# Last layer's end reordered in a four-layer attention stack: mixing, second keys, gating's last quarter, negated maxima, and the place of the loop edge

## What is computed

```python
kt = conv1x1(x, w_qk, b_qk)              # 1024 pixels
qt = conv1x1(xp, w_qk, b_qk)             # 256 pooled pixels
vt = conv1x1(xp, w_v, b_v)
pi = softmax(mix_weight @ mean(kt), over the 2 parts of a head)
attn = softmax(kt, over the 16 channels of a part) @ vt
attn = sum over the parts of (attn * pi) / sqrt(32)
out  = conv1x1(attn @ q, w_out)
x    = batch_norm(out) + x               # statistics over all 8 images
```

## Time and profile before

| what | value |
|---|---|
| median of 3 runs | 2867.67 us (2866.41 to 2867.95) |
| the profiled execution's own time | 2869.42 us |
| its span, first to last instruction | 2867.7 us |
| mean granted TensorE clock | 0.972 of full speed |
| PE busy | 93% of the span, 15892 matmuls |
| DVE, ACT, POOL busy | 70%, 45%, 24% |
| chain that ended last | PE 78%, DVE 9%, issue 5%, ACT 5%, DMA 1% |

### The profile page before, as it was taken

How to read it: one execution, slowest core, us unless ns; L and a number is a source line. 1 busy time by engine, 2 the same in 40 slices (tenths; PEclk the granted TensorE clock), 3 DMA queues, 4 the chain that set the end, 5 groups by cost and what they waited for, 6 DMA issues and landing times.

```text
span 2867.7 us, 44400 instructions
## 1 busy us (share of the span) xinstructions
PE 2657.3 (93%) x15892; PEld 1863.6 (65%) x15892; DVE 1996.5 (70%) x2297; ACT 1288.6 (45%) x1874; POOL 698.3 (24%) x444
## 2 busy tenths in 40 slices
PE   5899999999899999999989999999999999899994
PEld 4457775577655876567755777557775577656772
DVE  2766777766876768766776677775777666876666
ACT  2463435534365433644346343563335533365334
POOL 0540035300362013600236002440035300362001
PEclk7999999999999999999999999999999999999997
DMA  4300032000500005000050002300032000410007
GB/s 124 72 14 3 12 68 73 16 1 12 109 33 16 1 12 110 31 16 1 30 122 1 17 12 51 89 1 16 12 66 74 16 1 12 102 40 1 1 33 301
DMA packets 46237, 123.51 MB, mean 43 GB/s; under 512 B 9904, under 2 KB 21424, under 8 KB 42416
## 3 DMA queue, kind: packets, MB, share of 16 engines
q1 hardware_dynamic: 46000, 120.36, 15.6%
HBM read 41.96 MB, written 23.86 MB: 23 GB/s over the span
## 4 chain that ended last, share of the span: by engine, by line
PE 78%; DVE 9%; issue 5%; ACT 5%; DMA 1%; SPq 1%; DVEq 0%; ACTq 0%
PE tile L1539 23%; PE pv L1539 11%; PE tile L1625 9%; PE pv L1663 8%; PE tile L1653 6%; PE tile L1796 4%; PE tile L1689 4%; PE pv L1653 2%; PE tile L1818 2%; PE pv L1926 2%; PE tile L1847 2%; PE tile L1717 1%; DMA stack<-qk_r 1%; PE tile L1700 1%; ACT p L851 1%
## 5 line engine op out<-in xcount | busy, mean ns | idle before, releaser
L1120 DVE TENSOR_REDUCE small<-tile 128x1 f32<-128x1024 f32 x512 | 602.1, 1216 | 148.6 <-PE tile L1625 144.8
L851 ACT ACTIVATE p<-tile 128x512 f32<-128x512 f32 (+1 forms) x632 | 405.6, 689 | 228.9 <-PE tile L1653 227.3
L742 POOL TENSOR_TENSOR row_sum<-act 128x256 f32<-128x256 f32 x32 | 41.6, 1319 | 1478.6 <-DVE act L1313 1478.6
L1625 PE MATMUL tile<-stack 96*128 96x512 f32 x1024 | 361.3, 451 | 41.7 <-DVE small L1120 18.1
L1539 PE MATMUL tile<-qk_r 128*128 128x512 f32 x1536 | 377.9, 395 | 0.0
L712 POOL TENSOR_TENSOR acc<-acc,p 128x1024 f32<-128x1024 f32 x144 | 339.2, 2390 | 0.0
L1539 PEld LDWEIGHTS tile<-qk_r 128*128 128x128 f32 x1536 | 287.2, 188 | 66.4 <-issue 7.7
L1625 PEld LDWEIGHTS tile<-stack 96*128 96x128 f32 x1024 | 184.3, 198 | 214.5 <-issue 123.3
L1318 DVE TENSOR_TENSOR pl<-p,ph 128x1024 fp32r<-128x1024 f32 x128 | 158.2, 1236 | 220.9 <-ACT p L933 220.9
L1653 PE MATMUL tile<-stack 112*128 112x512 f32 x760 | 272.5, 425 | 3.8 <-ACT p L851 3.7
L1663 PE MATMUL pv<-p,v 128*32 128x512 f32 x2048 | 270.3, 604 | 1.4 <-ACT p L851 1.4
(11 more groups left out here) (284 smaller groups left out, 4514.6 us busy)
## 6 DMA issues: line engine op xcount, KB each, us to landing
stack<-qk_r SPq DMA_DIRECT2D x192, 256.0 KB, 5.0
x_in<-in_x_dram SPq DMA_DIRECT2D x8, 1024.0 KB, 4.9
act<-in_x_dram SPq DMA_DIRECT2D x8, 1024.0 KB, 4.7
x_scratch<-act SPq DMA_DIRECT2D x7, 1024.0 KB, 4.0
z_scratch<-act SPq DMA_DIRECT2D x7, 1024.0 KB, 5.4
stack<-ones SPq DMA_DIRECT2D x16, 256.0 KB, 4.7
w3f<-w3f_scratch SPq DMA_DIRECT2D x8, 512.0 KB, 3.3
fin_rest<-z_scratch SPq DMA_DIRECT2D x3, 1024.0 KB, 8.4
```

The costliest lines, as they stand in the source:

```text
L851: sc.activation(p0[:, jt % DEPTH, pair, first:first + len(heads) * HALF], tile_wait(batch, "st0", *u, jt, k), ACT.Exp, scale=float(D) ** - ...
L1120: ve.tensor_reduce(maxima[:, h * NT + it:h * NT + it + 1], t, X, ALU.max).then_inc(vector_done, vector.one("max0", g, h, it))
L1625: ins = mm(o[:, s], stack[0:IMAX, g, 0, h, it * P:(it + 1) * P], stack[0:IMAX, g, 1, h, s], start=True, stop=True)
```

## The change

- On PE the second keys, `qk0(1, 1)`, stand ahead of k = 7 instead of 6. The quarters of `z` stand ahead of k = 9, 11 and 14, and the last one behind all 16 score tiles. The first quarter waits for `g_kept` instead of `smt_kept`.
- On DVE `mixing` stands ahead of the maximum of k = 5 instead of 3.
- On ACT both `smt_kept` stand ahead of `g_kept`.
- The tile ring is set so that `m0` of the first unit has `tile2`; the two score tiles behind it take `tile0` and `tile1`. Before, `m0` had `tile1`, and the second of those score tiles waited for the readers of `m0`.
- The projections `qk_tiles(1)` and `v_tile(1, 0)` move from the end of a PE turn to the start of the next one: the edge of PE's loop lies between the 9 matmuls of `warm` and the queries.

```diff
     for layer in (1, 2):
-        s += [("v", 2, 0), ("v0", 0), ("v0", 1)] + [("qk", 2, t, ct) for t in range(2) for ct in range(CT)] if layer == 2 else []
+        s += [("v", 2, 0), ("v0", 0), ("v0", 1)] if layer == 2 else []
+        s += [("qk", layer, t, ct) for t in range(2) for ct in range(CT)] + ([("v", 1, 0)] if layer == 1 else [])
...
     for k in range(G * HT):
-        s += {1: [("mt",)], 2: [("qk0", 0, 1), ("g",)], 4: [("smt", 0), ("smt", 1)], 6: [("qk0", 1, 1)], 10: [("z", 0)],
-              14: [("z", 1)]}.get(k, [])
+        s += {1: [("mt",)], 2: [("qk0", 0, 1), ("g",)], 4: [("smt", 0), ("smt", 1)], 7: [("qk0", 1, 1)], 11: [("z", 0)]}.get(k, [])
         s += [("s0", *rows_of(UNITS[0], k))]
-    s += [("m0", *UNITS[0])]
+    s += [("z", 1), ("m0", *UNITS[0])]
...
         ring = ("scores" if kind in ("st0", "den0") else "rows") if looped else "whole"
+        if n == ("m0", *UNITS[0]):
+            rings[ring] = SLOTS - 1
...
                     smt_kept(0)
+                    smt_kept(1)
                     act_e.wait_ge(vector_done, vector.at(batch, "mix_pi"))
...
-                    smt_kept(1)
...
-                    if body and k == 3:
+                    if body and k == 5:
                         mixing()
...
-                        qk_tiles(2)
+                    qk_tiles(layer)
+                    if layer == 1:
+                        v_tile(1, 0)
...
                         if (ct, k) == (0, 0):
-                            scalar_wait("smt_kept", kt_)
+                            scalar_wait("g_kept", CT - 1)
...
-                    if head and k == 6:
+                    if head and k == 7:
                         qk0(1, 1)
-                    if body and k in (8, 10, 12, 14):
-                        z_half(*divmod(k // 2 - 4, 2))
+                    if body and k in (9, 11, 14):
+                        z_half(*{9: (0, 0), 11: (0, 1), 14: (1, 0)}[k])
                     if head:
                         s0(*rows_of(UNITS[0], k))
+                if body:
+                    z_half(1, 1)
                 if head:
                     m0(*UNITS[0])
...
                     warm(pv[:, 0:HALF], 9)
-                    qk_tiles(1)
-                    v_tile(1, 0)
```

More of the change, by code:

```diff
@@ L133, in tensor_steps @@
     s += [("ex0", *UNITS[-1]), ("out0", 1)]
-    return s + [("gn",), ("pv_groups",)] + [("qk", 1, t, ct) for t in range(2) for ct in range(CT)] + [("v", 1, 0)]
+    return s + [("gn",), ("pv_groups",)]
 def scalar_steps():
@@ L155, in scalar_steps @@
     s += [("qk0_hi", 0, 0), ("kt_exp", 0), ("qk0_hi", 1, 0), ("kt_exp", 1), ("qk0_hi", 0, 1), ("qk0_full", 0)]
-    s += [("mix_exp",), ("smt_kept", 0), ("g_kept", 0), ("g_kept", 1), ("smt_kept", 1)]
+    s += [("mix_exp",), ("smt_kept", 0), ("smt_kept", 1), ("g_kept", 0), ("g_kept", 1)]
     s += [("qk0_hi", 1, 1), ("qk0_full", 1), ("z_kept", 0), ("z_kept", 1)]
@@ L206, in vector_steps @@
         s += {1: [("mt_in",), ("kbar",), ("sm", 1)], 2: [("mix", n) for n in range(4)],
-              3: [("mix_sum",), ("mix_rec",), ("mix_pi",)]}.get(k, [])
+              5: [("mix_sum",), ("mix_rec",), ("mix_pi",)]}.get(k, [])
         s += [("max0", *rows_of(UNITS[0], k))]
@@ L265, in of_front, with of_norm @@
         "neg_hi", "neg_copy", "neg_lo") or name[0] in ("gn_dev", "gn")
-def of_projections(name):
-    return name in (("gn",), ("pv_groups",), ("v", 1, 0)) or name[0:2] == ("qk", 1)
+def of_norm(name):
+    return name in (("gn",), ("pv_groups",))
 class Steps:
@@ L319, in conv_seq_kernel @@
                     L3_bn_w, L3_bn_b, out):
-    tensor, scalar = Steps(tensor_steps(), of_first_layer, of_projections), Steps(scalar_steps(), of_first_layer)
+    tensor, scalar = Steps(tensor_steps(), of_first_layer, of_norm), Steps(scalar_steps(), of_first_layer)
     vector, gps = Steps(vector_steps(), of_first_layer, of_front), Steps(pool_steps())
```

## The result

The changed kernel takes **2836.39 us** (median of 4 runs, 2833.96 to 2843.89) against 2867.45 for the kernel before beside it (4 runs, 2866.41 to 2867.95): ratio 0.9897, 95% interval 0.9877 to 0.9916. It is faster by 31 us where 44 were forecast. The profiled execution took 2837.92, its span 2836.2 us, at a mean granted clock of 0.979. The four single runs lie 10 us apart. The four of the kernel before lie 1.5 apart, but in the larger groups beside the experiments (7 to 27 runs) that kernel's runs lie 4.9 to 7.3 apart, so the 1.5 is chance.

A forecast was written before the change was run, and what follows sets the result against it. PE is busy 93% of the span; the stretch before `m0` was taken as bound by DVE's waits and PE's order together. Terms -42.0 - 0.8 - 2.4 + 1.0 = -44.2 take 2867.67 to 2823.5 us, range 2815 to 2841.

The forecast's parts named there:

- seven turns up to the exp of jt = 2: Loop turns: exp comes 6.0 us sooner each (bounds 5.2 and 6.6), capped by the stack DMAs; -42.0 in seven.
- first turn, with its start: First turn, without mixing or `z`: ring gives 1.0, stack DMAs land up to 1.0 later; -0.8 (bounds -1.0 and +0.5).
- loop edge: PE's loop jump moved to where PE idles 1.25 us anyway: 3.0 gained, 0.6 sticking out; -2.4 (bounds -3.0 and +4).
- last turn: `g_kept` stands behind a second `smt_kept` of 1.03, and PE's first `z` quarter waits for `g_kept`: +1.0.
- A: As rival (0.10): half-clock stretch around `m0` shrinks, turn gains 6.6, 2819; as time: SP's first issue of first group's stack DMAs.
- so the last landed near 444.8, then 3.8 ahead of the exp: Stack DMAs before the change: last landing read from DMA shares, 3.8 us ahead of the exp at 448.59.
- B: Rival (0.16): clock still falls under the second keys, DMAs land 1.7 later, turn gains 4.3; 2835.5.
- C: Rival (0.07): the loop jump is dear at its new place, +4 instead of -2.4; 2830.
- D: Rival (0.03): half clock throughout PE's `z` stretch, +25 in seven turns; 2890, the slower side.
- E: Rival (0.06): half the gain is lost to an unseen wait in the first units, 3.0 a turn; 2844.5.
- F: Rival (0.02): the order does nothing, or only 2.6 counts, as DMAs already held the exp; 2850 to 2867.
- later in the order, sooner in time: Second keys on PE: start after tile 4's maximum, end at 421.0 against 423.74, 2.6 us sooner; stack DMAs likewise.

The follow-up runs named there:

- experiment 1: Kernel before with the ring line alone (`m0` into `tile2`): 2870.18 us, ratio 1.0001 to the kernel before.
- experiment 9: Changed kernel with six matmuls that nothing reads where PE waits for the exp of jt = 2: 2837.81 us, ratio 0.9892 to the kernel before.
- experiment 7: Changed kernel with one more 256 KB stack DMA (ones rows written again) in the second series: 2869.6 us, ratio 0.9999 to the kernel before.
- experiment 5: Kernel before with all moves of the order, without ring line and moved loop edge: 2839.38 us, ratio 0.9903 to the kernel before.
- experiment 4: Kernel before with the mixing later, both `smt_kept` ahead of `g_kept`, first `z` quarter waiting for `g_kept`: 2848.69 us, ratio 0.9924.
- experiment 8: Changed kernel with its second keys ahead of tile 6 again instead of 7: 2826.18 us, ratio 0.9848 to the kernel before.
- experiment 10: Kernel before with the new order, second keys ahead of tile 6, without ring line and moved edge: 2842.42 us, ratio 0.9907.
- experiment 11: Kernel before with the new order, second keys ahead of tile 6, and ring line, edge not moved: 2831.83 us, ratio 0.987.
- experiment 12: Changed kernel, second keys ahead of tile 6, plus unread matmuls in the last turn ahead of `mt` and first `z` quarter: 2826.67 us, ratio 0.9858.

## Why the prediction was right, and where its size was off

The faster side and the range held; the forecast was 13 us too low. Its terms against the two profiles, in us:

| Term | forecast | in the traces |
|---|---|---|
| seven turns up to the exp of jt = 2 | -42.0 | -39.0 |
| clock behind the new wait | none | +6.0 |
| first turn, with its start | -0.8 | -1.9 |
| loop edge | -2.4 | -2.9 |
| last turn | +1.0 | +6.2 |
| remainder | | +0.1 |
| sum | -44.2 | -31.5 |

Of the 13 us, 6.0 are the clock behind the new wait, 5.2 the last turn and 3.0 the turn's cap; the edge and the start give 1.6 back.

**Right, step by step.** The mixing was held by POOL, at 0.15 now. The second keys' DMAs start 24.5 behind A instead of 26.9 on average in turns 1 to 6: 2.4, forecast 2.6. `m0` comes 4.7 to 5.1 sooner in turns 1 to 6; forecast 5.6, from a turn that was itself 1.5 longer than the others (its `mt` stretch ran at half clock), so it comes 6.7 sooner there. `st0` stands 2.30 behind `m0`, forecast 2.3. ACT waits for stack DMAs at jt = 2, as foretold. The edge gave 2.9 where 2.4 were forecast. Ahead of the row scores no gap stands now, and the 0.54 us behind their first eight matmuls stood in the unrolled turn before as well. At the first jump's new place PE idles 1.23 us for the normalised input, before 1.25; at the other five 1.26 to 1.76, so something of the jump does stick out, as forecast. It costs nothing, since the negated maxima stand 30.0 us behind the group norm in every turn. From the timelines of PE and DVE:

```profile
563.98 0.73 PE L1542 MATMUL tile<-xh,w_1qh 128*128 128x512 f32 x2 [1.23 <-ACT xh L886]
...
580.98 6.85 PE L1801 MATMUL tile<-qk_r 128*128 128x512 f32 x24 [0.54 <-DVE vl L1226]
```

```profile
590.30 0.16 DVE L1134 SCALAR_TENSOR_TENSOR small<-small,mh 128x8 f32<-128x8 f32 x1
```

By the forecast's own signs, a turn shortened by less than 5 would have been wrong. From A to the next A it is shortened by 5.0, up to the exp by 5.6: it kept clear of that by a hair.

**The step that failed: "so the last landed near 444.8, then 3.8 ahead of the exp".** That was read from a DMA share of 0.37 over two microseconds, as if the DMAs had run at full share and then stopped. The trace of before has the landing. First, for the last of the twelve DMAs, issued at 440.69, the time from issue to landing; then the windows (columns as in the earlier trace rows):

```profile
DMA to landing us min/median/max: 5.7/5.7/5.7
```

```profile
445.00:445.50 0.50, 0.50 (x3) 0.40 (x2) 0.50 (x1) 0.29 (x1) 0.00 (x0) 0.50 0.06 8
445.50:446.00 0.50, 0.50 (x3) 0.42 (x2) 0.50 (x1) 0.50 (x2) 0.00 (x0) 0.75 0.04 16
446.00:446.50 0.50, 0.50 (x3) 0.19 (x1) 0.26 (x2) 0.31 (x2) 0.13 (x1) 1.00 0.00 0
```

The DMAs trail off with shares of 0.06 and 0.04, and the last one lands at 440.69 + 5.7 = 446.4. That is 2.2 ahead of the exp, not 3.8; in the seven turns of the loop it was 2.2 to 3.2. In the changed kernel the chain of waits shows the landing (columns: start, length, what):

```profile
434.86 4.74 DMA stack<-qk_r
439.60 0.02 issue
```

The same reading of its window (0.39 from 438 to 440) would have said 438.8. From the series' first issue to the last landing it took 17.4 to 18.4 us in the loop before and 17.0 to 17.2 after; the exp starts 0.2 behind. So the turn's gain of 5.6 is made of three parts: 2.6 by which the series starts sooner (2.4, and the 1.5 of turn 0 spread over seven), 2.3 of room (2.5 on average, less that 0.2), and 0.8 by which the series itself was quicker; 0.1 is lost by turn 2, where the clock held the exp. The forecast didn't have the last, and it isn't the order that gives it: experiment 1, with the old order, has 17.1 to 17.7. The execution that the forecast read happened to land late. That is luck for the number, some 5 us over seven turns: without it the turn would have gained some 4.8, not the forecast 6.0. The wait was forecast, at the right instruction, and its size was read too favourably by 1.6 in the turn that was read.

**What wasn't charged: the clock behind a wait that the forecast itself set up.** It put the exp on the DMAs and priced the wait as a wait. In three of seven turns PE's idle 1.5 to 1.7 us were followed by half clock, 1.5 or 3.0 us more each. In experiment 9 the fall is gone where the gap is filled, in experiment 7 it is there in every turn, where the wait is longer. Why it fell in three turns and not in three others stays open. The spread between runs may have the same source: it is 10 to 15 us in the kernels whose exp waits for the DMAs while PE idles (the changed one, experiments 5 and 7) and 3 to 6 in experiments 4 and 8 to 12. Most of these are four runs each, so it isn't shown.

**The last turn.** The +1.0 is there to the digit: from the transposes' end to the first quarter 1.94 instead of 0.97. Timeline of PE:

```profile
2784.87 1.74 PE L1899 MATMUL pv<-qv 128*128 128x128 f32 x8 [2.09 <-DVE qv L1416]
...
2791.41 3.65 PE L1922 MATMUL tile<-ident,kt 128*128 128x128 f32 x16
2797.00 3.67 PE L1931 MATMUL pv<-smt,g_pi 128*128 128x512 f32 x8 [1.94 <-ACT g_pi L990]
```

But from `mt` to the end of the transposes it took 10.19 us, before 5.91: 4.3 more, at half clock, with the waits of 2.09 and 0.74 that before had too. From the last negated maxima to the end it took 203.6 us before, 209.8 now, and 206.9 to 211.1 in all runs with the new order; but experiment 1, with the old order, has 207.8 as well. The other microsecond of the 6.2 lies ahead of `mt`. What brings the clock down there stays open. And the forecast's +1.0 was a wait without its clock: in six of the nine profiles with the later mixing, half clock followed this wait of 1.9 us, and from the first quarter to the end it took 1.6 more (40.9 for 39.3). In the changed kernel's profile it happened not to.

**The rivals.** A's mechanism came true in six of seven turns: no half clock behind `m0`. In this kernel it gave nothing beyond the cap, because the DMAs held the exp, which is what A said, with too high a cap. B's number, 2835.5, is close to the result and its mechanism didn't happen: the clock is at 1.00 under the second keys, with the transposes still in front of them. The Trainium skill, TensorE: Matmul & The Clock Gate, section Part 4: PE-mode transpose, says of a transpose that "it doesn't count as PE-busy the same way". The traces neither confirm nor refute that; they show that the transposes alone did not bring the clock down here: experiment 4 takes the idle time away, and the fall goes with it. C and D didn't happen. E foresaw a turn shortened by half, 3.0; it is 4.7 with everything. F is out: the order alone gives 0.9903. The keys "later in the order, sooner in time" hid a price: the move from tile 6 to 7 took 1.0 us from the chain that bound next. The forecast named that chain and didn't ask whether this part of the change helped it; without it the kernel takes 2826.2. That this is close to the forecast for the change as a whole is chance: it is another kernel, whose last turn still loses 4.0 us where the forecast had 1.0.

## What to carry to other kernels

When a change brings a consumer forward until it meets a transfer, take the transfer's landing from its issue and the time to landing (here 440.69 + 5.7), not from the DMA share of a window, and start the transfer sooner before moving anything else: 1 us on that path was worth 10 here. Charge an idle gap on PE twice, for itself and, as a chance, for the half clock that may follow (here 1.5 or 3.0 us in three of six turns). Don't judge parts of a change one by one in the old order alone: the ring line gave 0 there and, with the keys at 6, 10.6 us in the new one.

## What the runs showed that wasn't expected

- The same gap of 1.5 to 1.7 us on PE was followed by half clock in turns 0, 3 and 4 and not in 1, 5 and 6. With waits of 0.92 and 1.16 us around `m0` the clock fell in six of seven turns (experiment 10), and in five of seven in experiment 5; with 0.91 and 0.78 in none of 21 with the keys at 6 (experiments 8, 11 and 12), but in six of 21 with the keys at 7 (one in the changed kernel, three in experiment 7, two in experiment 9). So the length of the two waits alone doesn't decide it.
- Matmuls brought forward into a stretch at half clock gain almost nothing: 0.95 us at `st0` left 0 to 0.4 at the exp (experiment 1).
- One DMA more of 256 KB in pieces of 512 bytes, 1.19 us in SP's queue like its neighbours with their rows of 4 KB, moved the last landing by 2.7 us (experiment 7).
- The same twelve DMAs landed 17.0 to 17.2 us behind their first issue in one kernel and 17.4 to 18.4 in another. Why stays open.
- An addition of 128x2 on DVE takes 0.15 us alone and 1.65 beside a POOL subtraction of 2.35 us, in which it ends 0.02 us behind it.
